# Edge counts of two relations in one weighted pass, placed between the bias rows and the query product

## The reference

```python
def _rgcn(x, W_rel, W_root, bias, src, dst, etype):
    xr = jnp.einsum('ni,rio->rno', x, W_rel)
    msg = xr[etype, src]
    out = x @ W_root + bias
    for r in range(NUM_RELATIONS):                       # 3
        m = etype == r
        s = jax.ops.segment_sum(jnp.where(m[:, None], msg, 0.0), dst, num_segments=n)
        c = jax.ops.segment_sum(m.astype(x.dtype), dst, num_segments=n)
        out = out + s / jnp.maximum(c, 1.0)[:, None]
    return out
...
qg = jnp.einsum('blf,gf->blg', q, Wg[:, F:]) + bg
```

## Time and profile before

| | us |
|---|---|
| median of 3 runs | 1258.62 (1258.33 to 1262.88) |
| the profiled execution, device time | 1258.37 |
| its span | 1256.6 |
| TensorE busy | 1118.9 (89%) |
| VectorE busy | 733.8 (58%) |
| ScalarE busy | 548.8 (44%) |
| GpSimd busy | 131.6 (10%) |

### The profile page before, as it was taken

One profiled execution on the slowest core, in us unless ns is written; L12 is line 12 of the kernel. 1 busy time (PEld: TensorE's weight loads), 2 busy tenths in 40 slices (PEclk: granted clock), 3 DMA queues, 4 the chain that ended last, 5 costly groups with the idle time before them and its releaser, 6 DMA issues. The chain is left out here.

```text
span 1256.6 us, 17142 instructions
## 1 busy us (share of the span) xinstructions
PE 1118.9 (89%) x7246; PEld 921.1 (73%) x7246; DVE 733.8 (58%) x1049; ACT 548.8 (44%) x575; POOL 131.6 (10%) x84
## 2 busy tenths in 40 slices
PE   7999997999879869999579887878999999999986
PEld 6888874445779745448458787854899999999973
DVE  6583447887043158881343464324688888888851
ACT  0221017886032258880123353222566666666630
POOL 2020003554000015550000000000000000000000
PEclk9999997999979989999799888968999999999998
DMA  8044235220323451212224202410877777777720
GB/s 266 1 150 150 76 109 150 61 68 18 118 108 119 136 148 51 66 37 76 76 76 151 76 1 76 173 50 1 272 256 241 248 234 255 233 258 232 257 79 26
DMA packets 82192, 162.66 MB, mean 129 GB/s; under 512 B 4034, under 2 KB 60126, under 8 KB 81822
## 3 DMA queue, kind: packets, MB, share of 16 engines
q1 hardware_dynamic: 80720, 151.86, 36.2%
q0 software_dynamic: 1392, 9.66, 2.9%
HBM read 157.86 MB, written 0.80 MB: 126 GB/s over the span
## 5 line engine op out<-in xcount | busy, mean ns | idle before, releaser
L1533 DVE TENSOR_TENSOR Wlo<-W,Whi 128x2304 fp32r<-128x2304 f32 x68 | 173.7, 2556 | 43.4 <-ACT Whi L1134 43.4
L1134 ACT CAST Whi<-W 128x2304 fp32r<-128x2304 f32 x68 | 144.2, 2122 | 0.0
L851 PE MATMUL PS<-Whi,Mhi 128*128 128x384 f32 x408 | 139.6, 342 | 3.5 <-DVE Mlo L1562 3.5
L618 PE MATMUL PS<-QH,SEL 128*128 128x512 f32 x384 | 118.7, 433 | 23.0 <-DVE QH L1324 15.3
L851 PE MATMUL PS<-Wlo,Mhi 128*128 128x384 f32 x408 | 136.5, 335 | 0.0
L851 PE MATMUL PS<-Whi,Mlo 128*128 128x384 f32 x408 | 136.5, 335 | 0.0
L392 POOL TENSOR_TENSOR PRDP<-arena 128x1024 f32<-128x1024 f32 x48 | 114.5, 2386 | 103.2 <-PE PS L634 83.6
L618 PEld LDWEIGHTS PS<-QH,SEL 128*128 128x128 f32 x384 | 67.4, 195 | 74.2 <-DVE PRD L1348 22.7
L1015 ACT ACTIVATE arena<-PS 128x1024 f32<-128x1024 f32 x96 | 98.5, 1026 | 34.5 <-PE PS L618 34.5
L1015 ACT ACTIVATE PS<-PS 128x1024 f32<-128x1024 f32 x96 | 97.9, 1020 | 0.0
L851 PEld LDWEIGHTS PS<-Whi,Mhi 128*128 128x128 f32 x408 | 76.8, 188 | 8.3 <-DVE Mlo L1562 8.3
(11 more groups left out here) (233 smaller groups left out, 2186.4 us busy)
## 6 DMA issues: line engine op xcount, KB each, us to landing
W<-in_L_rel SPq DMA_DIRECT2D x68, 1152.0 KB, 5.6
W<-in_W_rel SPq DMA_DIRECT2D x6, 2304.0 KB, 8.7
W<-in_W SPq DMA_DIRECT2D x6, 2304.0 KB, 8.4
arena<-in_qU SPq DMA_DIRECT2D x96, 128.0 KB, 2.6
W<-in_WqT SPq DMA_DIRECT2D x4, 2304.0 KB, 9.1
W<-in_W_root SPq DMA_DIRECT2D x2, 2304.0 KB, 14.0
W<-in_WgT SPq DMA_DIRECT2D x2, 2304.0 KB, 8.4
QH<-QH POOLq DMA_DIRECT2D x2, 1536.0 KB, 9.9
```

The lines of the kernel that those rows point to most:

```text
L618: mm = pe.matmul(PS[:, 2 * (c % 3) + b // 2, :], SEL[:, i, :], QH[h][:, u, b:b + 2, :].rearrange("p b f -> p (b f)"), start=True, stop=True)
L851: mm = pe.matmul(PS[:, 4 + s % 2, 0:HALF], MS[a][mb][:, k, j * P:(j + 1) * P], WS[b][w % 3][:, k, :], start=n == 0, stop=n == 17)
L1134: nc.scalar.copy(WS[0][w % 3][:], W[(FIRST34 + r) % 2][:, :, q * HALF:(q + 1) * HALF]).then_inc(w_hi, 1)
L1533: V.tensor_tensor(WS[1][w % 3][:], W[(FIRST34 + r) % 2][:, :, q * HALF:(q + 1) * HALF], WS[0][w % 3][:].bitcast(F32), ALU.subtract).then_i ...
```

## The change

The edges of relations 0 and 1 are counted in one pass. Edge keys no longer ask for one type: an edge of type 0 gets weight 1, an edge of type 1 weight 4096, an edge of type 2 key 0. The sum of a cell is then c0 + 4096 c1; bf16 holds both weights exactly, and the fp32 sum is exact. VectorE splits the sum again: it takes 1024 off and divides by 4096, rounds by adding and taking off 12582912, and subtracts 4096 times the result from the sum.

The pass is issued between the bias rows and the first query half, and chunk by chunk: VectorE writes S1 and E[1] of a chunk one after the other and counts it in `chunk_ready`; TensorE waits for each chunk and does its two matmuls. The chunks of the first half (17) go to bank 6, those of the second to bank 7, so that VectorE splits one while the other is filled. Relation 2 keeps its own pass, behind the first query half. The spread of relations 0 and 1 becomes one product of 512 columns. ScalarE no longer copies counts 0 and 1. The wait for qg_ready 8 becomes one for 4 before the product with W_root1 (banks 0 to 2) and one for 8 before the `offs` matmul, which writes bank 4.

```diff
+STEP = 4096.0
+ROUND = 12582912.0
+EHALF = EC // 2
...
+            for c in range(EC):
+                h, i = divmod(c, EHALF)
+                pe.wait_ge(chunk_ready, c + 1)
+                for s in range(NT):
+                    mm = pe.matmul(PS[:, 6 + h, s * NODES:(s + 1) * NODES], S1[:, c, s * P:(s + 1) * P], E[1][:, c, :],
+                                   start=i == 0 and s == 0, stop=i == EHALF - 1 and s == NT - 1, skip_group_check=True)
+                if i == EHALF - 1:
+                    mm.then_inc(cnt_summed, 1)
...
-            for r in range(R3):
-                if r == 0:
-                    pe.wait_ge(s1_ready, 1)
-                counts(r, r % 2, bank=6)
-                if r < 2:
-                    if r == 0:
-                        pe.wait_ge(q_in[1], 16)
-                    mm = natural3(qT[1], W[0], bank=3, last=True, tiles=[r])
-                    if r == 1:
-                        mm.then_inc(w_used, 1)
-                spread_counts(r, CNT[:, r], bank=7)
-            pe.wait_ge(qg_ready, 8)
+            pe.wait_ge(cnt_copied, 2)
+            for s in range(NT):
+                mm = pe.matmul(PS[:, 7, :], ones[:], CNT[:, 0:2, s, :], start=s == 0, stop=s == NT - 1)
+            mm.then_inc(deg_spread, 2)
+            counts(2, 0, bank=6)
+            pe.wait_ge(q_in[1], 16)
+            natural3(qT[1], W[0], bank=3, last=True, tiles=[0])
+            spread_counts(2, CNT[:, 2], bank=7)
+            natural3(qT[1], W[0], bank=3, last=True, tiles=[1]).then_inc(w_used, 1)
+            pe.wait_ge(qg_ready, 4)
...
+                        pe.wait_ge(qg_ready, 8)
...
-            for r in range(R3):
-                if r:
-                    t = r - 1
-                    act.wait_ge(q_done if t == 0 else w_used, 1)
-                    for j, h in product(range(2), range(2)):
-                        nc.scalar.copy(query_rows(0, t, j, h), query_sums(t, j, h)).then_inc(qg_hi, 1)
-                counts_copy(r, CNT[:, r], bank=6)
+            for t in range(NT):
+                act.wait_ge(q_done if t == 0 else w_used, 1)
+                for j, h in product(range(2), range(2)):
+                    nc.scalar.copy(query_rows(0, t, j, h), query_sums(t, j, h)).then_inc(qg_hi, 1)
+                if t == 0:
+                    counts_copy(2, CNT[:, 2], bank=6)
...
-            onehot(S1[:], keyf[:, 0, :]).then_inc(s1_ready, 1)
-            for r in range(R3 + 1):
-                if r < R3:
-                    then(V.scalar_tensor_tensor(out=ekey[:, r % 2, :], in0=keyf[:, 2, :], scalar=float(r), in1=keyf[:, 1, :],
-                                                op0=ALU.is_equal, op1=ALU.mult))
-                    if r == 2:
-                        dve.wait_ge(cnt_summed, 1)
-                    onehot(E[r % 2], ekey[:, r % 2, :]).then_inc(e_ready, 1)
...
+            then(V.scalar_tensor_tensor(out=ekey[:, 0, :], in0=keyf[:, 2, :], scalar=1.5, in1=keyf[:, 1, :], op0=ALU.is_lt, op1=ALU.mult))
+            then(V.tensor_scalar(ekey[:, 1, :], keyf[:, 2, :], STEP - 1.0, 1.0, ALU.mult, ALU.add))
+            for c in range(EC):
+                V.tensor_scalar(S1[:, c, :], iotab[:], keyf[:, 0, c:c + 1], None, ALU.is_equal)
+                V.tensor_scalar(E[1][:, c, :], iotab[:], ekey[:, 0, c:c + 1], ekey[:, 1, c:c + 1], ALU.is_equal, ALU.mult
+                                ).then_inc(chunk_ready, 1)
+
+            dve.wait_ge(chunk_ready, EC)
+            for h in range(2):
+                dve.wait_ge(cnt_summed, h + 1)
+                both = PS[:, 6 + h, :].rearrange("p (s n) -> p s n", s=NT)
+                low, high = (CNT[:, 0], CNT[:, 1]) if h == 0 else (NRM[:, 1], NRM[:, 2])
+                then(V.tensor_scalar(NRM[:, 0], both, STEP / 4, 1.0 / STEP, ALU.subtract, ALU.mult))
+                then(V.tensor_scalar(high, NRM[:, 0], ROUND, ROUND, ALU.add, ALU.subtract))
+                then(V.scalar_tensor_tensor(out=low, in0=high, scalar=-STEP, in1=both, op0=ALU.mult, op1=ALU.add))
+            V.tensor_tensor(CNT[:, 0], CNT[:, 0], NRM[:, 1], ALU.add).then_inc(cnt_copied, 1)
+            V.tensor_tensor(CNT[:, 1], CNT[:, 1], NRM[:, 2], ALU.add).then_inc(cnt_copied, 1)
+            then(V.scalar_tensor_tensor(out=ekey[:, 0, :], in0=keyf[:, 2, :], scalar=2.0, in1=keyf[:, 1, :], op0=ALU.is_equal, op1=ALU.mult))
+            onehot(E[0], ekey[:, 0, :]).then_inc(e_ready, R3)
+            onehot(E[1], keyf[:, 1, :]).then_inc(d1_ready, 1)
...
+            normalise_counts(0)
+            normalise_counts(1)
+            query_lo(0)
             dve.wait_ge(cnt_summed, R3)
...
+            normalise_counts(2)
...
+            query_lo(1)
```

More of the change, by code:

```diff
@@ L228, in build @@
         sel_ready, s1_ready, e_ready = sem("sel_ready"), sem("s1_ready"), sem("e_ready")
+        chunk_ready = sem("chunk_ready")
         cnt_summed, cnt_copied = sem("cnt_summed"), sem("cnt_copied")
@@ L893, in _ @@
             with pe.Else():
-                pe.wait_ge(s1_ready, 2)
+                pe.wait_ge(s1_ready, 1)
                 counts(R3, 1, S1=S1L)
```

37 lines of the change are left out of this document (17 added, 20 removed).

## The result

The changed kernel takes 1251.66 us, median of 9 runs (1249.04 to 1254.17). The kernel before, run beside it on the same chip, takes 1262.01 us (9 runs, 1258.33 to 1266.79). The ratio is 0.9921, 95% interval 0.9904 to 0.9938. The profiled execution has a span of 1249.9 us and a device time of 1251.66 us, against 1256.6 and 1258.37 before.

The account below looks back on a forecast made before the run. The first stage was taken as bound by the sum of TensorE's work, so savings there reach the end whole. Terms -7.53 - 0.96 - 1.20 = -9.7 us gave a median of 1248.9 us, range 1246.0 to 1253.0.

Parts of the forecast that it names:

- One pass fewer: TensorE's count passes: three become two, 68 matmuls of 0.111 us saved, -7.53 us.
- The shared pass in 9.3 us: Pass ahead of the query product: 7.53 plus 1.8 for the low-rate start, ending at 26.9; 0 net.
- The chunks: VectorE's 34 one-hot pairs at 0.40 us each: all stand at about 21.6, 5 us ahead of TensorE; cost 0.
- 34 waits: TensorE's waits on chunk_ready in the shared pass: a wait already met costs nothing inside a block; 0.
- Spread: Spread of both relations: 4 records of 512 columns, 1.7 us, against two of 0.86 before; 0.
- The two waits at the end: Third relation's spread no longer waits for ScalarE's copy, -0.96; the W_root1 product not for the second low part, -1.20.
- What is late next: Work behind the first stage (normalising, low parts, W_rel 0, transfers): all ready before it is wanted; nothing late.
- The sum: First stage's end: -9.7 us, moving the start of the product with W_root1 from 77.31 to 67.6.
- the gain shrinks later: Later stretches of low granted clock: 1.8 us each, two going against it make +3.6, 1252.5 us; chance 0.09.
- The level not lifted: Shared pass on one-hot operands does not raise TensorE's clock level: +7.0, 1255.9 us; chance 0.07.
- the pauses at the waits: TensorE pauses 0.33 us at each of 34 waits and stays at the low level: +18.2, 1267.1 us; chance 0.04.
- the slow one-hot: VectorE's new one-hot takes 0.42 us, so the shared pass ends at about 29.5: +2.6, 1251.5 us; chance 0.04.

## Why the prediction was right, step by step

The median of 1251.66 us lies in the range of 1246.0 to 1253.0, and the change is faster, as forecast; the sum holds to 0.1 us at the end of its stage and is 3 us too good at the end of the span. That the median fell into the range is in part luck: the same kernel's other two medians are 1252.86 and 1253.22 us, one just inside the upper end and one just outside.

**One pass fewer, -7.53.** Held. One pass put back costs 7.7 us at L425 and 7.5 in the span.

**The shared pass in 9.3 us.** It took 8.98, 9.65 and 9.84 us; in the first of these profiles the level rises 3.4 us into it (17.6 to 20.9), in the others after 4.8 and 5.2. As forecast, the low start is only handed from the query product (15.43 us now) to the pass, and one-hot operands lift the level as well as full ones. The 3.7 us of full matmuls that I counted ahead of the rise before were nearer 3.4: the last one with the full 634 ns starts at 20.27 us, and from 21.05 on they take 380 ns.

**The chunks.** Mis-sized, without effect. I took 0.2 us for the new one-hot, by L1288, and 0.40 a chunk. Measured are 0.26 and 0.45:

```profile
9.18 0.28 DVE L1240 TENSOR_SCALAR S<-iotab,keyf 128x256 bf16<-128x256 bf16 x1
9.37 0.35 DVE L1241 TENSOR_SCALAR E<-iotab,ekey 128x256 bf16<-128x256 bf16 x1
9.63 0.29 DVE L1240 TENSOR_SCALAR S<-iotab,keyf 128x256 bf16<-128x256 bf16 x1
...
17.92 0.67 DVE L1241 TENSOR_SCALAR E<-iotab,ekey 128x256 bf16<-128x256 bf16 x1
```

L1288 has two operators but one pointer, and it was the second pointer that cost. The last chunk stood at 23.4 us, not at 21.6. TensorE reached it at 26.6, so 3 us of cover were left of the 5 that I counted. The 0.67 is a chunk beside GpSimd's DMA issues of xN and xT (16.48 to 18.57), 0.3 more than its neighbours, as the 7.04 against 6.75 in the earlier trace rows had it. The Trainium skill, SBUF — State Buffer, section "SBUF: two separate sides", has GpSimd and a VectorE operation in one of its two-port modes exclude each other at a shared port pair. Two of the ten or so operations beside these two issues are long here (0.67 and 0.48 us), which agrees in kind; in which mode they ran no run shows.

**34 waits, 0.** Held: with one wait the pass takes 9.49 us, no less, and the matmuls start at the same distances.

**Spread, 0.** Held: from the spread's first matmul to that of the pass behind it, 42.21 to 43.92, are 1.71 us, as forecast. The 0.24 us that TensorE's weight loads idle ahead of each other there cost nothing, as the matmuls of 512 columns last longer than the loads.

**The two waits at the end, -0.96 and -1.20.** Held: no releaser stands at L468 or L425 any more.

**What is late next: nothing.** Held. The split ends at 30.15 (forecast 31), NRM of relation 2 at 66.2 (68), the low parts at 76.5 (77), all before they are wanted; W_rel is asked for at 67.95 (68), and L490 starts at 83.08 (83.0) without a wait.

**The sum, L425 at 67.6.** It stood at 67.54, and at 68.24 and 68.38 in the other two profiles.

**From there to the end.** This is the step that was off, and the rival "the gain shrinks later" came partly true: 6.7 us of 9.7 at the end of the first pair of profiles, 7.7 of 9.6 in the mean of three. I priced it at 1.8 us for each stretch and named the mechanism as the place where the clock rises; measured was 2.5 us for one group that a low stretch hits or misses. What I had not seen is how much of this happens with no change at all: up to 5.2 us between profiles of the kernel before. The single profile of before had a device time (1258.37) under the medians measured later (1259.8 to 1262), and so was a favourable one to make the sum against. The predicted median leaned on it, too: a ratio from the sum, 1248.9 / 1258.6 = 0.9923, is next to the measured 0.9921 and 0.1 to 0.2% too good against 0.9934 and 0.9944.

**The rivals that did not come.** The level not lifted, the pauses at the waits, the slow one-hot of 0.42 us: none of them in this order. The first is real, though, in the kernel with bias rows between the chunks.

## What to carry to other kernels

Work saved on the engine that binds a stage arrives at the next stage whole (7.5 us for a pass of 7.5), if the result is used late enough: put the merged step early and other work between it and its reader, or the unpacking becomes a wait (3.65 us and 4.68 us here), and the waiting lowers the clock on top. Where the clock has still to rise, matmuls that use one partition cost twice as much, and mixed between the others they went with a level that did not rise; a short block of them in the midst of full work ran at the high rate. Before a difference of a few microseconds is explained by the program, profile each kernel more than once: two profiles of one kernel were 5 us apart here, 2.5 of it in one group that a low-rate stretch hit in one of them. Then look for a group that tells the courses apart, and compare profiles of the same course.

## What the runs showed of the hardware

- Within a block of matmuls on one partition (the bias rows), behind a pass with pauses, the granted clock went from 0.99 to 0.50 with TensorE busy all the time: 374 ns for the first ones, 629 ns from 26.8 us on, 2.3 us into their block. A block of 2.85 us in the version with half of them later did not lower it. What tells the two apart, the length of the block or the slower work ahead of it, was not tried.
- Matmuls on one-hot operands lifted the level 3.3 to 5.2 us into a pass (5.7 behind two waits of VectorE's work). At the high level a pass that had matmuls under way in 8.67 of 10.30 us held it.
- A second pointer operand costs VectorE 0.06 us in an operation of 128x256 bf16 elements; a second operator costs nothing.
- The granted clock of the windows reads 1.00 in the first 20 us while the matmuls take their longer duration, and up to 37 us in the version with bias rows between the chunks. The duration is what is to be read there.
- One unedited kernel takes two courses: a group of 24 matmuls of 128x8 near 700 us lasts 2.85 us at a granted clock of 1.00 or 5.29 us at 0.50, and profiles with the first kept their distance at L425 to the end of the span within 0.4 us.
